# The key projection of a cross-attention block: one product of three parts per half instead of four tripled ones, its copies laid out by transfers

## The reference, cut to what matters

```
x    [16, 256, 128]   queries' side,   ctx [16, 64, 128]   keys' side,   mask [16, 64]
q = shape(layernorm(x) @ Wq) * 8**-0.5      # 16 heads of 8
k = shape(ctx @ Wk);  v = shape(ctx @ Wv)
attn = softmax(q k^T + (1 - mask) * finfo.min)
x = x + (attn v) @ Wo
x = x + moe(layernorm(x))                   # 8 experts, top 2 of softmax(x @ gate.T),
                                            # capacity 640, silu(x Wg) * (x Wu) @ Wo
```

## Time and profile before

| | us |
|---|---|
| median of 3 runs (lowest, highest) | 383.05 (382.66, 383.46) |
| the profiled execution, its own time | 382.68 |
| its span, first to last instruction | 380.7 |
| PE busy | 345.0 (91%) |
| DVE busy | 254.6 (67%) |
| ACT busy | 193.7 (51%) |
| POOL busy | 229.1 (60%) |

### The profile page before, as it was taken

How to read it: one execution, slowest core, us unless ns; L and a number is a source line. 1 busy time by engine, 2 the same in 40 slices (tenths; PEclk the granted TensorE clock), 3 DMA queues, 4 the chain that set the end, 5 groups by cost and what they waited for, 6 DMA issues and landing times.

```text
span 380.7 us, 9057 instructions
## 1 busy us (share of the span) xinstructions
PE 345.0 (91%) x3017; PEld 302.5 (79%) x3017; DVE 254.6 (67%) x981; ACT 193.7 (51%) x443; POOL 229.1 (60%) x195
## 2 busy tenths in 40 slices
PE   5889879898999997399999999999999999999970
PEld 1566667677877864288999999999999999999970
DVE  4999999999999997524455565645546455465440
ACT  3577777787878875224333444444434343443320
POOL 6383636575666567740663775755748748378663
PEclk9999999999999999689999999999999999999996
DMA  5898402222323121124237345363463643734232
GB/s 180 245 339 272 140 9 56 77 50 68 84 63 108 46 71 58 58 72 114 22 29 177 28 80 126 36 161 42 39 167 34 130 71 34 176 28 37 25 32 21
DMA packets 41158, 34.33 MB, mean 90 GB/s; under 512 B 8336, under 2 KB 37520, under 8 KB 40976
## 3 DMA queue, kind: packets, MB, share of 16 engines
q1 hardware_dynamic: 26592, 23.67, 21.4%
q0 software_dynamic: 13568, 9.58, 18.4%
q10 hardware_dynamic: 960, 0.60, 0.5%
HBM read 21.12 MB, written 17.73 MB: 102 GB/s over the span
## 4 chain that ended last, share of the span: by engine, by line
PE 64%; DVE 20%; issue 4%; POOL 4%; DMA 3%; ACT 2%; SPq 1%; POOLq 1%; DVEq 0%; ACTq 0%
PE bank L915 18%; PE bank L672 10%; PE bank L674 9%; PE bank L673 9%; DVE mneg L1021 5%; PE bank L775 5%; POOL slots L437 3%; PE bank L743 3%; PE bank L766 2%; DVE xn L1002 2%; DVE stats L988 2%; PE bank L906 2%; DVE rall L1071 2%; DMA maskr<-in_mask 1%; POOL out L471 1%
## 5 line engine op out<-in xcount | busy, mean ns | idle before, releaser
L471 POOL DMA_INDIRECT out<-ys,idx x80 | 125.4, 1568 | 82.2 <-DVE ys L1301 29.6
L1328 DVE TENSOR_TENSOR h<-sg,bank 128x256 f32<-128x256 f32 x160 | 66.0, 418 | 86.5 <-ACT sg L657 79.3
L657 ACT ACTIVATE sg<-bank 128x256 f32<-128x256 f32 x160 | 61.6, 385 | 107.2 <-PE bank L674 106.4
L672 PE MATMUL bank<-ex_hi,w_hi 128*128 128x256 f32 x320 | 95.5, 298 | 1.0
L674 PE MATMUL bank<-ex_lo,w_hi 128*128 128x256 f32 x320 | 89.1, 278 | 0.0
L673 PE MATMUL bank<-ex_hi,w_lo 128*128 128x256 f32 x320 | 89.0, 278 | 0.0
L437 POOL DMA_INDIRECT slots<-rall,slot x64 | 62.9, 983 | 34.0 <-DVE slot L1177 20.6
L915 PE MATMUL bank<-w_raw,h 128*128 128x128 f32 x640 | 78.0, 275 | 0.8 <-DVE h L1328 0.8
L915 PEld LDWEIGHTS bank<-w_raw,h 128*128 128x128 f32 x640 | 74.9, 192 | 1.0 <-DVE h L1328 1.0
L672 PEld LDWEIGHTS bank<-ex_hi,w_hi 128*128 128x128 f32 x320 | 60.3, 188 | 4.3 <-issue 2.5
L673 PEld LDWEIGHTS bank<-ex_hi,w_lo 128*128 128x128 f32 x320 | 60.4, 189 | 0.0
(11 more groups left out here) (122 smaller groups left out, 535.9 us busy)
## 6 DMA issues: line engine op xcount, KB each, us to landing
slots<-in_empty SPq DMA_DIRECT2D x8, 660.0 KB, 11.0
xl<-slots SPq DMA_DIRECT2D x7, 660.0 KB, 7.1
w_raw<-in_wgu SPq DMA_DIRECT2D x8, 512.0 KB, 3.8
w_raw<-in_wdn SPq DMA_DIRECT2D x8, 256.0 KB, 4.3
out<-X SPq DMA_DIRECT2D x16, 128.0 KB, 1.9
X<-in_x SPq DMA_DIRECT2D x3, 512.0 KB, 5.3
out<-ys,idx POOLq DMA_INDIRECT x80, 3.3
slots<-rall,slot POOLq DMA_INDIRECT x64
```

What stands on the lines that cost most here:

```text
L471: nc.gpsimd.indirect_dma_start(out=out[:, :], out_offset=bass.IndirectOffsetOnAxis(ap=IDX[v][:, j:j + 1], axis=0), in_=YS[c][:, t, :], in_ ...
L657: nc.scalar.activation(SG[m % 2][:], GATE_PS[m % 2][:, 0:2 * P], ACT.Silu).then_inc(sg_ready, 1)
L672: nc.tensor.matmul(ps, hi, m_hi, start=True, stop=False)
L1328: nc.vector.tensor_tensor(H[n % 2][:, f, :], SG[m % 2][:], UP_PS[m % 2][:, 0:2 * P], ALU.mult).then_inc(h_ready, 1)
```

## The change

The weight WK is now 128 columns wide, with its columns permuted so that column 4c+g is column c of group g. `project_keys(half)` makes all four groups of half the batches at once: three matmuls 128 x 128 against 512 columns. ScalarE copies the 128 rows over `CTXM` (the high part) and VectorE writes the difference over `CTX_LO`. From these two tiles transfers lay out the three parts: for batches 0 to 5 into `KC`, now [row, group, batch, key], by three transfers for batches 0 and 1 and three for 2 to 5; for batches 6 to 15 into a new tile `KL` [row, batch, group, key], by twelve transfers for the keys and four for the mask row. All of these are on SyncE's list. Two of the four mask rows of KC go by ScalarE. Several pieces of work change their place in the lists. The diff, with context left out:

```diff
@@ -136,17 +136,17 @@
-        NW = GROUPS * 96
...
-        WK = s1("wk", [P, NW])
-        WK_HI = s1("wk_hi", [P, NW], F32R)
-        WK_LO = s1("wk_lo", [P, NW], F32R)
+        WK = s1("wk", [P, D])
+        WK_HI = s1("wk_hi", [P, D], F32R)
+        WK_LO = s1("wk_lo", [P, D], F32R)
...
-        KC = s1("kc", [P, B, GROUPS, LK])
+        KC = s1("kc", [P, GROUPS, KBUF, LK])
+        KL = s1("kl", [P, B - KBUF, GROUPS, LK])
@@ -203,7 +203,7 @@
-        K_PS = [MX[0], MX[1], DEN_PS, M1, M1, M1, M1, M1]
+        K_PS = M1
@@ -221,6 +221,8 @@
+        kc_in = [sem(f"kc_in{v}") for v in range(2)]
+        kl_in = sem("kl_in")
@@ -312,22 +314,33 @@
-            for g in range(GROUPS):
-                sp.dma_start(KC[ONE_ROW:ONE_ROW + 1, :, g, :], EXT[:]).then_inc(ext_in, 16)
+            for g in range(2):
+                sp.dma_start(KC[ONE_ROW:ONE_ROW + 1, g, :, :], EXT[0:KBUF, :]).then_inc(ext_in, 16)
+            def arrange_keys(piece):
+                b0, b1 = ((0, 2), (2, KBUF))[piece]
+                sp.wait_ge(k_used, 1)
+                for part in range(3):
+                    keys = CTXM[:, b0:b1, :] if part < 2 else CTX_LO[:, b0 * LK:b1 * LK].bitcast(F32)
+                    sp.dma_start(KC[32 * part:32 * part + 32, :, b0:b1, :], keys).then_inc(kc_in[piece], 16)
+            arrange_keys(0)
+            arrange_keys(1)
...
-                b = slice(2 * j, 2 * j + 2)
+                b = slice(2 * j - KBUF, 2 * j - KBUF + 2)
...
-                        sp.dma_start(KS[rows, to, :, h * LK:(h + 1) * LK].bitcast(F32), KC[rows, b, :, :]).then_inc(done, 16)
+                        sp.dma_start(KS[rows, to, :, h * LK:(h + 1) * LK].bitcast(F32), KL[rows, b, :, :]).then_inc(done, 16)
@@ -340,8 +353,14 @@
-            sp.wait_ge(k_used, 8)
-            sp.wait_ge(ext_in, 64)
+            sp.wait_ge(k_used, 2)
+            for part in range(3):
+                for g in range(GROUPS):
+                    keys = CTXM[g:P:GROUPS, KBUF:, :] if part < 2 else CTX_LO[g:P:GROUPS, KBUF * LK:].bitcast(F32)
+                    sp.dma_start(KL[32 * part:32 * part + 32, :, g, :], keys).then_inc(kl_in, 16)
+            for g in range(GROUPS):
+                sp.dma_start(KL[ONE_ROW:ONE_ROW + 1, :, g, :], EXT[KBUF:, :]).then_inc(kl_in, 16)
+            sp.wait_ge(kl_in, 16 * 16)
@@ -383,7 +402,7 @@
-                nc.gpsimd.memset(KC[ONE_ROW:, 8 * half:8 * half + 8, :, :], 1.0).then_inc(kc_set, 1)
+                nc.gpsimd.memset(KC[ONE_ROW:, :, 3 * half:3 * half + 3, :], 1.0).then_inc(kc_set, 1)
@@ -402,7 +421,7 @@
-                    KC[0:NROW, i].unsqueeze(2).to_broadcast([NROW, GROUPS, HG, LK]),
+                    KC[0:NROW, :, i, :].unsqueeze(2).to_broadcast([NROW, GROUPS, HG, LK]),
@@ -415,7 +434,7 @@
-            pool.wait_ge(k_used, 4)
+            pool.wait_ge(kc_in[0], 48)
@@ -440,6 +459,7 @@
+                    wait(pool, kc_in[1], 48)
@@ -494,14 +514,10 @@
-            def keys_hi(n):
-                half, g = n // 4, n % 4
-                act.wait_ge(k_full, n + 1)
-                if n == 0:
-                    act.wait_ge(kc_set, 2)
-                nc.scalar.copy(KC[0:96, 8 * half:8 * half + 8, g, :].bitcast(F32R),
-                               K_PS[n][0:96, :].rearrange("p (b k) -> p b k", k=LK)).then_inc(k_hi, 1)
+            def keys_hi(half):
+                act.wait_ge(k_full, half + 1)
+                nc.scalar.copy(CTXM[:, 8 * half:8 * half + 8, :].rearrange("p b k -> p (b k)").bitcast(F32R), K_PS[:]).then_inc(k_hi, 1)
@@ -576,15 +592,17 @@
-            for n in range(4):
-                keys_hi(n)
+            act.wait_ge(ext_step, 2)
+            act.wait_ge(kc_set, 2)
+            for g in range(2, GROUPS):
+                act.dma_start(KC[ONE_ROW:ONE_ROW + 1, g, :, :], EXT[0:KBUF, :]).then_inc(ext_in, 16)
+            keys_hi(0)
+            keep_values(0)
...
-            keep_values(0)
+            keep_values(1)
...
-            context_hi(1)
...
-            keep_values(1)
@@ -593,8 +611,8 @@
-                if i in (0, 1):
-                    keys_hi(2 * i + 4)
+                if i == 1:
+                    keys_hi(1)
@@ -610,8 +628,8 @@
-                if i in (0, 1):
-                    keys_hi(2 * i + 5)
+                if i == 0:
+                    context_hi(1)
@@ -678,17 +696,13 @@
-            def project_keys(n):
-                half, g = n // 4, n % 4
+            def project_keys(half):
...
-                if n == 0:
-                    pe.wait_ge(wk_lo_ready, 1)
-                if n >= 4:
-                    pe.wait_ge(k_used, n)
+                pe.wait_ge(wk_lo_ready, 1)
+                wait(pe, k_used, half)
...
-                w = slice(96 * g, 96 * g + 96)
-                product3(K_PS[n][0:96, :], WK_HI[:, w], WK_LO[:, w], CTX_HI[:, cols], CTX_LO[:, cols]).then_inc(k_full, 1)
+                product3(K_PS[:], WK_HI[:], WK_LO[:], CTX_HI[:, cols], CTX_LO[:, cols]).then_inc(k_full, 1)
@@ -829,14 +843,13 @@
-            for n in range(4):
-                project_keys(n)
+            project_keys(0)
+            pe.wait_ge(any_ready, 1)
+            project_values(0)
...
-            pe.wait_ge(any_ready, 1)
-            project_values(0)
@@ -854,8 +867,8 @@
-                if i in (0, 1):
-                    project_keys(2 * i + 4)
+                if i == 1:
+                    project_keys(1)
@@ -880,8 +893,6 @@
-                if i in (0, 1):
-                    project_keys(2 * i + 5)
@@ -973,12 +984,11 @@
-            def keys_lo(n):
-                half, g = n // 4, n % 4
-                dve.wait_ge(k_hi, n + 1)
-                lo = KC[64:96, 8 * half:8 * half + 8, g, :]
-                nc.vector.tensor_tensor(lo.bitcast(F32R), K_PS[n][64:96, :].rearrange("p (b k) -> p b k", k=LK), lo, ALU.subtract).then_inc(k_used, 1)
+            def keys_lo(half):
+                dve.wait_ge(k_hi, half + 1)
+                nc.vector.tensor_tensor(CTX_LO[:, 512 * half:512 * half + 512], K_PS[:],
+                                        CTXM[:, 8 * half:8 * half + 8, :].rearrange("p b k -> p (b k)"), ALU.subtract).then_inc(k_used, 1)
@@ -1179,23 +1189,19 @@
+            context_lo(0)
+            moments(0)
...
-            context_lo(0)
-            moments(0)
...
-            for n in range(1, 4):
-                keys_lo(n)
...
-            mask_context(1)
...
-            context_lo(1)
@@ -1210,8 +1216,8 @@
-                if i in (0, 1):
-                    keys_lo(2 * i + 4)
+                if i == 0:
+                    mask_context(1)
@@ -1253,8 +1259,10 @@
-                if i in (0, 1):
-                    keys_lo(2 * i + 5)
+                if i == 0:
+                    context_lo(1)
+                if i == 1:
+                    keys_lo(1)
@@ -1356,11 +1364,6 @@
-    def stacked(w):
-        g = w.reshape(D, GROUPS, 1, 32)
-        return np.ascontiguousarray(np.broadcast_to(g, (D, GROUPS, 3, 32)).reshape(D, GROUPS * 96))
@@ -1368,7 +1371,7 @@
-        "wk": stacked(a["L0_xattn_Wk"]),
+        "wk": np.ascontiguousarray(a["L0_xattn_Wk"].reshape(D, GROUPS, 32).transpose(0, 2, 1).reshape(D, D)),
```

## The result

The changed kernel takes 385.44 us (median of 14 runs, 383.81 to 390.32), the kernel before 382.64 (14 runs beside it, 381.81 to 384.40). The ratio is 1.0068, 95% interval 1.0051 to 1.0085; two of the 14 runs of the changed kernel (390.32 and 389.84) were in a slower state of the chip, and the ratio leaves them out. Forecast was 381.1, range 379.8 to 383.8. The profiled execution took 383.81 us with a span of 382.0, 1.13 more than the profiled one of before; it is the fastest of its 14, so what it shows is less than what the median lost.

What follows compares the result with a forecast made beforehand. Until 88 us the prediction took VectorE's chain, with GpSimd in it, to bound the kernel. A gain of 1.9 us there by step 1 gave 383.05 - 1.9 = 381.15, so 381.1; range 379.8 to 383.8.

Steps and rivals of the forecast that it cites:

- Preamble, keys: Key product, high copy and difference in the preamble: they end at 12.3 us; ScalarE's two mask-row issues taken at 0.6 each.
- Preamble, transfers: SyncE's three copies for batches 0 and 1: landed 1.9 us after issue, at 15.5, when GpSimd's first spread starts.
- Preamble, VectorE: 4.5 us of VectorE work leaves the preamble; the first maximum starts at 18.05 instead of 19.70, 1.65 us earlier.
- TensorE's clock falls: Rival, chance 0.24: over 3 us without TensorE work before norm(0) lowers its clock; a short fall leaves half the gain, 382.1.
- low for 10: Longer case of the clock rival: low clock for 10 us, at most half of them, 5 us, lost; up to 386.
- one gap only: Argument against the clock rival: TensorE has a single gap in the preamble, and the work behind it is dense.
- Batches 6 to 15: SyncE's late key transfers: KL landed at 51 us, place_keys(3) at 64.8, batch 6 row scores at 67; cover 2.2 us.
- The late keys: Rival, chance 0.14: place_keys(3) lands after row_scores(6, 0) wants it; each us late is lost; priced at 384.5.
- GpSimd holds: Rival, chance 0.12: mask_context(1) held until the second spread too; 1.5 us of the gain goes, 382.6.

Runs made afterwards that it cites:

- The filler kernels: The changed kernel plus twelve unused matmuls on TensorE between the first values and first turn, run on two chips: ratios 0.9962 and 0.9981 to the kernel before.
- e2_weights_late: The changed kernel with the spare zeros and first two experts' weights loaded behind the place_keys loop instead of ahead of the KL transfers: ratio 1.0006 to the kernel before.
- h2_after: The changed kernel, unedited, run beside the kernel before on another chip: ratio 1.0013 to the kernel before.
- i2_fill4: The changed kernel with zeros and first weights loaded late and 4 unused TensorE matmuls before the first turn: ratio 0.9939 to the kernel before.
- f4_late_keys_first: The changed kernel with late weights and ScalarE's high key copy ahead of its mask rows, no filler: ratio 0.9865 to the kernel before, three runs.

## Why the prediction was wrong

- **"Preamble, keys"**: right. 12.3 forecast, 12.27 measured, but by two errors that cancel: the context landed 0.85 us earlier with the smaller weight (its mask starts at 4.76 to 5.23 in all kernels with the change, at 5.45 to 5.72 in all without), and ScalarE's two issues took 1.99 instead of 1.2.
- **"Preamble, transfers"**: nearly right. The last copy landed 2.3 us after its issue instead of 1.9, and the spread started 0.5 late.
- **"Preamble, VectorE"**: wrong, 20.64 for 18.05. This is the step that failed. It took the selected queries to be ready at 17.6, from durations at 2.4 GHz. The filler kernels put them there: 18.44 and 18.54, then 26.54 and 26.64 for batch 1 (26.2 forecast) and 34.43 and 34.52 for batch 2 (34.5). With the clock held the steps come out within 0.5 us. In the changed kernel it was 1.2 GHz from 12.5 to 22.7, the scores came late, and VectorE waited 2.73 us for them.
- **The rival "TensorE's clock falls"** named the gap, its length and its place, and had 0.24. Its price was the error: as one number it took a short fall of some 3 us, of which "GpSimd's chain covers most", and 382.1. Falls of 3.4 us (e2_weights_late and h2_after) put the first maximum at 19.34 and 19.71, 0.8 to 1.3 behind the fillers. On the first chip the fall lasted 10.2 and took all of the 1.9. That is the rival's other case, "low for 10", up to 386, which had no part in the price. It also took "one gap only" as an argument against, where i2_fill4 (longest wait 2.56) and the first fall of f4_late_keys_first show that thin work without a gap of 3 us is followed by a fall too.
- **"Batches 6 to 15"**: the cover of 2.2 us was called thin, and wasn't there. The 0.76 an issue left out that an issue itself can stall while the queue's backlog drains. The transfers started at 36.45 instead of 34 and took 21.2 us instead of 17, so KL came 6.7 us later than the 51 taken. So the rival "The late keys" (0.14) came as well, though its 384.5 was too dear: queries at 69.87 also came late, and only 0.7 us was lost.
- **"GpSimd holds"**: half. mask_context(1) took 1.75 instead of 0.69 and ended at 25.85, behind the spread's 23.40 + 1.90, as its like in the earlier trace rows. What that cost by itself was not measured.
- The sum for the profiled span: 1.9 us of gain that did not come, 0.2 lost by batch 5, 0.7 by batch 6 and 0.4 in the experts' stage make the 3.2 us between 378.8 (380.7 less 1.9) and 382.0. The first and second have the clock's fall as their cause, the third the late keys by the chain alone, the fourth is open.
- What no run explains: the median of the changed kernel is 1.6 us above its profiled execution. Executions with more falls may do it (h2_after's had three and took 408.99, its median is 407.65), but no slower execution on the first chip was traced.

## What to carry to other kernels

When a change takes work out of an engine's list, ask what TensorE does in the place that becomes empty: it may lose its full clock there, and then the durations of the old trace don't hold for the matmuls behind it. Check that against the wait that is next, since a low clock costs only where TensorE is what others wait for. And count a transfer's issue by what stands ahead of it in its queue, not by the price it has in a quiet one.

## What the runs showed of the hardware

- The clock fell without a long idle time too: in i2_fill4 at 14.9, after waits of at most 2.56 us, in f4_late_keys_first at 12.1, after one of 0.95 and inside one of 1.25.
- The same program fell at different times and for different lengths: with the weights late from 11.8 to 18.6 once, from 13.5 to 16.9 once; the changed kernel from 12.5 to 22.7 and from 14.4 to 17.8.
- The kernel before reached 2.4 GHz by 9.58 us in one execution (matmuls of 0.39 us) and at 12.7 in another. The Trainium skill (TensorE: Matmul & The Clock Gate, "What's actually happening") says that the number of slow matmuls at a kernel's start varies from run to run; these two executions agree.
- A SyncE issue of a transfer between two SBUF tiles took 0.60 us in the preamble (13.67) and up to 4.98 behind the weights' loads.
- Two issues of a mask row by ScalarE took 1.99 us, 1.0 each, where SyncE's two took 1.60.
